# Cross attention by long convolution and a routed FFN on one core: count loads spread over the gathers, store ahead of the read-back, places behind a product

## What is computed

```python
x = x + long_convolution(layernorm(x), k, bias, ctx, ctx)      # stage 1
xt = layernorm(x).reshape(2048, 256)                           # stage 2: 16 experts, 4 a token
scores = softmax(xt @ Wg.T)
topi = 4 best experts within the 2 best groups of 4
h = silu(xt @ W1[e]) * (xt @ W3[e])                            # inner width 176
y = sum over the 4 chosen e of scores[e] * (h @ W2[e])
z = (silu(xt @ Ws1.T) * (xt @ Ws3.T)) @ Ws2.T                  # shared expert, width 352
x = x + y + z
```

## Time and profile before

| | us |
|---|---|
| median of 3 runs | 414.01 |
| lowest and highest of them | 413.64, 414.26 |
| the profiled execution's own time | 410.32 |
| its span, first to last instruction | 408.6 |

### The profile page before, as it was taken

How to read it: one execution, slowest core, us unless ns; L and a number is a source line. 1 busy time by engine, 2 the same in 40 slices (tenths; PEclk the granted TensorE clock), 3 DMA queues, 4 the chain that set the end, 5 groups by cost and what they waited for, 6 DMA issues and landing times.

```text
span 408.6 us, 9369 instructions
## 1 busy us (share of the span) xinstructions
PE 395.1 (97%) x2144; PEld 292.9 (72%) x2145; DVE 241.7 (59%) x663; ACT 168.0 (41%) x513; POOL 185.1 (45%) x231
## 2 busy tenths in 40 slices
PE   7999999999999999999999999999999999999994
PEld 6788788788888445555877777777676767677772
DVE  3576577898978447674344444464646464646464
ACT  5348557555653640111234334333343433333341
POOL 3253333338887644646463333333333333333344
PEclk9999999999999999999999999999999999999999
DMA  7964664468869996454443333646364645454662
GB/s 238 368 232 144 204 223 143 144 243 295 283 222 379 322 315 203 147 217 154 141 148 117 110 110 109 200 134 211 124 213 134 201 146 189 158 192 154 219 222 98
DMA packets 39421, 79.71 MB, mean 195 GB/s; under 512 B 5792, under 2 KB 26624, under 8 KB 37344
## 3 DMA queue, kind: packets, MB, share of 16 engines
q1 hardware_dynamic: 32528, 59.57, 44.5%
q0 software_dynamic: 6864, 19.80, 12.5%
HBM read 54.95 MB, written 24.40 MB: 194 GB/s over the span
## 4 chain that ended last, share of the span: by engine, by line
PE 69%; DVE 8%; DMA 7%; SPq 5%; issue 5%; POOL 3%; ACT 1%; DVEq 1%; POOLq 0%
PE heads L1189 17%; PE bank L1251 13%; PE heads L1097 9%; PE heads L1229 8%; PE bank L1241 5%; DMA toep<-rows_scratch 4%; PE heads L1099 4%; PE bank L1208 4%; DVE kv L636 3%; PE heads L1199 3%; PE bank L1111 3%; SPq L324 2%; DVE prod L665 2%; POOL rows_scratch L563 2%; DMA toep<-toep_in 2%
## 5 line engine op out<-in xcount | busy, mean ns | idle before, releaser
L617 POOL DMA_INDIRECT y_scratch<-toep,dest_i x79 | 76.6, 969 | 119.0 <-DVE dest_i L962 106.0
L1189 PE MATMUL heads<-w,toep 128*128 x316 | 106.6, 460 | 0.0
L1251 PE MATMUL bank<-w,toep 88*128 x316 | 82.0, 381 | 0.5 <-DVE toep L932 0.5
L563 POOL DMA_INDIRECT rows_scratch<-rows,slot_i x64 | 63.4, 991 | 38.9 <-issue 19.1
L1097 PE MATMUL heads<-toep,kv 128*128 128x256 f32 x256 | 77.8, 386 | 2.4 <-DVE kv L636 1.7
L1189 PEld LDWEIGHTS heads<-w,toep 128*128 128x128 f32 x316 | 53.8, 190 | 17.0
L458 ACT ACTIVATE toep<-heads 128x176 f32<-128x176 f32 x79 | 25.0, 317 | 82.9 <-PE heads L1189 82.9
L1251 PEld LDWEIGHTS bank<-w,toep 88*128 88x128 f32 x316 | 53.7, 190 | 6.1 <-issue 1.2
L932 DVE COPY toep<-heads 88x256 f32<-88x256 f32 x79 | 33.2, 421 | 37.9 <-PE heads L1199 37.8
L1099 PEld LDWEIGHTS heads<-toep,kv 128*128 128x128 f32 x256 | 48.6, 190 | 6.6
L665 DVE TENSOR_TENSOR prod<-heads,ctx_rep 128x1024 f32<-128x1024 f32 x32 | 39.0, 1219 | 22.2 <-PE bank L1111 19.8
(11 more groups left out here) (158 smaller groups left out, 439.8 us busy)
## 6 DMA issues: line engine op xcount, KB each, us to landing
ctx_rep<-ctxr_in SPq DMA_DIRECT2D x16, 1024.0 KB, 4.9
toep<-rows_scratch SPq DMA_DIRECT2D x79, 144.0 KB
prod<-y_scratch SPq DMA_DIRECT2D x7, 1024.0 KB, 5.2
w<-w_in SPq DMA_DIRECT2D x16, 352.0 KB
w<-w_in SPq DMA_DIRECT2D x16, 176.0 KB
rows_scratch<-pad_row SPq DMA_DIRECT2D x17, 144.0 KB
ctx_tr<-ctxt_in SPq DMA_DIRECT2D x16, 128.0 KB, 5.0
toep<-toep_in SPq DMA_DIRECT2D x4, 512.0 KB, 7.1
```

The costliest lines, as they stand in the source:

```text
L563: pool.indirect_dma_start(rows_d, bass.IndirectOffsetOnAxis(ap=slot_i[:, u, k:k + 1].bitcast(U32), axis=0), rows[:, u, :], None).then_inc( ...
L617: pool.indirect_dma_start(y_d, bass.IndirectOffsetOnAxis(ap=dest_i[b][:, 0:1].bitcast(U32), axis=0), y_sb[b], None).then_inc(y_sent[b], 16)
L1189: last = nc.tensor.matmul(up_ps[p], x_tr[p][:, blk, :], w13[:, bass.ds(e, 1), blk, :].rearrange("p a n -> p (a n)"), start=blk == 0, stop= ...
L1251: last = nc.tensor.matmul(dn_ps[p], hid_tr[p][:, c, :], w2[:, bass.ds(e, 1), c, :].rearrange("p a n -> p (a n)"), start=c == 0, stop=c == 1)
```

## The change

Two parts, independent of each other.

1. In SP's loop over m = 4 to 8, each of the gathers 8m to 8m + 3 is followed by the load of one of the four counts of sends. Behind them come the store and then the read-back, which finds its counts in registers and only waits and issues its DMA. Before, the store stood behind the gather 8m + 1, and the four loads and the read-back behind the gather 8m + 2. The other read-backs load their counts as before.
2. On DVE, `places(3)` stands behind `hidden_shared(5)` rather than ahead of it.

```diff
-            def read_back(i, u0, units, into, signal):
-
-                sends = [sp.value_load(tile_row[0:1, bass.ds(i * DEPTH + (TILES + b), 1)],
-                                       min_val=16, max_val=16 * (TILES // DEPTH)) for b in range(DEPTH)]
+            def sends_of(i, b):
+
+                return sp.value_load(tile_row[0:1, bass.ds(i * DEPTH + (TILES + b), 1)],
+                                     min_val=16, max_val=16 * (TILES // DEPTH))
+
+            def read_back(i, u0, units, into, signal, sends=None):
+
+                if sends is None:
+                    sends = [sends_of(i, b) for b in range(DEPTH)]
                 for b in range(DEPTH):
                     sp.wait_ge(y_sent[b], sends[b])
...
             with sp.Fori(4, 9) as m:
-                gathers(m, 0, 2)
+                sends = []
+                for b in range(DEPTH):
+                    gathers(m, b, b + 1)
+                    sends.append(sends_of(m - 3, b))
                 store(m - 4, m * 2 - 8, 2)
-                gathers(m, 2, 3)
-                read_back(m - 3, m * 2 - 6, 2, back, back_in)
-                gathers(m, 3, 8)
+                read_back(m - 3, m * 2 - 6, 2, back, back_in, sends)
+                gathers(m, 4, 8)
...
             marks(3)
+            hidden_shared(5)
             places(3)
-            hidden_shared(5)
             dve.wait_ge(counted, 1)
             slot_of_expert(3)
```

## The result

The changed kernel takes 417.98 us, the median of 5 runs (416.46 to 418.60), against 414.15 for the kernel before (5 runs, 413.64 to 415.31, the three of the table above among them). The ratio is 1.0083, with a 95% interval of 1.0056 to 1.0110: slower by 3.4 us (2.3 to 4.6), where the prediction had 0.9 and a range that ended at 416.7. The profiled execution spans 414.7 us, against 408.6.

The account below looks back on a forecast made before the run. The prediction took PE, busy for 97% of the span, to bound the kernel. Part 1's +0.25 us and part 2's 0.64 gave +0.9 on a median of 414.01, so 414.9 us, with a range of 412.5 to 416.7.

Parts of the forecast that it names:

- 3.5 us: Time PE loses over tiles 33 to 73, the five turns m = 4 to 8, 0.70 a turn.
- U: Start of the up product of tile 8m + 1; the turn's first add was forecast at U + 4.85.
- Restarting PE costs some 0.1 more: In each turn, PE's restart behind the late first add was put at 0.1 us beyond the lateness of 0.6.
- So 0.75 a turn: PE's loss in each turn under part 1, 0.70 to 0.80 us; 3.75 for five against 3.5 before.
- the first add must start by U + 4.23: Latest start of DVE's first add in a turn for copy_h to be ready for PE's down product.
- The 0.03 us of room: Before the change, DVE's first add in turn m = 4 starts at U + 4.20, against a limit of U + 4.23.
- up to 0.35: PE's restart behind the wait for the gather in turn m = 4, 1.01 lost less 0.66 us idle.
- PE loses another 0.64 us: Part 2: places(3) delays add_z(2), so PE waits 0.64 us longer ahead of the twelve down products.
- 0, if something on DVE gave way: Lower bound of part 2's cost ahead of the twelve down products; the upper was 0.75 us.
- The send is caught: Rival: POOL's send falls behind the read-back and place(33) waits for it; +2.65 us, 416.7, chance 0.17.
- The read-back fits: Rival: in the turns, DVE's late adds go unseen by PE or the read-back lands sooner; -1.9 us, 412.1, chance 0.20.
- Places hidden: Rival: PE's wait ahead of the twelve down products doesn't grow; +0.25 us, 414.3, chance 0.08.

Follow-up runs that it names:

- Experiment 3: Part 1 alone with DVE's four adds one step later: 0.9920 of the kernel before; the same adds on the kernel before: 1.0165.
- Experiment 5: PE loads the next tile's expert number earlier: on part 1 alone 0.9999 of the kernel before, on the kernel before 0.9964.
- part 1 alone: SP's loop as changed, places(3) at its old place, against the kernel before: 1.0059, 415.35 against 412.82 us.
- experiments 2 and 4: Part 1 alone, with store behind read-back: 1.0091 of the kernel before; loads paired behind two gathers: 0.9999; read-back ahead of gather 8m + 3: 0.9927.

## Why the prediction was wrong

*Right.* The bound was found: the 3.5 us lie in the turns, and behind PE's wait for the gather stands a second chain over DVE that ends at nearly the same time. Part 1 takes the first away and makes the second longer; PE's idle time moves from the turning (L1208) to the down product (then L1251, now L1258); the gather leaves 1.04 us behind `take`, where 1.1 was predicted; the first add starts at U + 4.92 on the mean, where U + 4.85 was. Experiment 3 confirms the chain: with the add off it, nothing is lost. That the add came within 0.07 us of its forecast is partly luck, see below.

*Wrong, and the step that failed: "Restarting PE costs some 0.1 more", "So 0.75 a turn".* The lateness of 0.6 was right (0.69 measured), the restart wasn't: 0.58 us beyond the lateness, 1.27 a turn. The price was taken from the twelve down products at 168.96, behind which no register is loaded. In a routed step PE's program loads an expert's number behind the stalled product. In the changed kernel that load and the step behind it cost 0.46 a turn (1.54 us from down product to up product rather than 1.18, and 0.10). Experiment 5 takes the load from behind the stall, and this cost is gone.

*A second error in the same step, "the first add must start by U + 4.23".* The due time left out the 0.24 us from the end of the copy to the loading of the weights. With it and the 1.92 in place of 2.05 it is U + 4.12, so the mean add was 0.80 late and not 0.69: 0.80 + 0.46 = 1.26 of the 1.27 that a turn loses. The 0.03 us of room was read from one turn as well. In the same trace the first adds of the other four turns start at U + 3.80, 4.06, 3.85 and 3.66.

*The nearer price.* The row that was nearest in kind was in sight: the stall for the gather cost "up to 0.35" beyond its idle time, and even that was set aside. In the five turns part 1 comes to +2.8 us on the two profiled executions, or +2.3 on the means of the profiles, in place of +0.25; part 1 alone measured +0.59% (0.32% to 0.86%), which is 1.3 to 3.6 us.

*Too small a sample: 3.5 us as what before loses.* A second profile loses 4.7. This goes the other way, and makes the surprise smaller, not larger.

*Part 2, "PE loses another 0.64 us".* In the first two profiles the wait grew by 0.89 (0.51 to 1.40), in all of them on the mean by 0.34 (1.06 to 1.40), and alone it measured 1.0004 (0.9988 to 1.0020), which holds both nothing and 0.64. The direction was right. The size was wrong because the execution that was read had the smallest wait of ten, with no gap on DVE at all; the bound "0, if something on DVE gave way" was the better half of the truth.

*A term that came out by two errors.* The read-back's issue was to start at U - 0.75 and, with the 0.38 us of the earlier trace rows, to end at U - 0.37. It ends within 0.03 us of U in all five turns, 0.35 to 0.4 later. (Its row starts at U - 0.53 and is 0.53 us long in one turn, and starts at U - 0.03 to U and is 0.02 long in the others; part 1 alone has both kinds with the same ends, so the end is the figure to go by.) SP's rows before it are in place: the store leaves 1.33 us behind the gather, where 0.65 + 0.35 + 0.34 had been put. In return the first add comes 4.65 to 4.87 us behind that end in four turns, rather than 5.6 - 0.38 = 5.2, and 5.48 behind it in turn m = 4. The read-back's packets take 3.5 to 3.7 us from first to last in these four turns, 3.4 to 3.8 in the kernel before, and 4.35 in turn m = 4: the overlap with the store, put at 0.3 a turn, shows in one turn alone. Why the issue ends later was not tried.

*The rivals.* "The send is caught" had the nearest size (416.7, inside the measured interval), but by luck, since its cause wasn't there: `place(33)` didn't wait. It did in experiments 2 and 4, where the read-back left before the send or within 0.1 us behind it. The prediction compared the ends of the two issues, where the starts of the packets decide: 1.54 us behind the send's row and 1.04 behind the read-back's. "The read-back fits" was wrong, as the add came 0.4 us or more behind even the U + 4.23. The 0.03 us of room that was named against it was the reading of one turn. "Places hidden" is what part 2 nearly does. The sum with the numbers measured since, +2.3 for part 1 and +0.34 for part 2, is +2.6, inside the measured interval of 2.3 to 4.6; the remaining 0.8 to its middle isn't accounted for.

## What to carry to other kernels

When two chains end within a few tenths of each other, relieving one gains nothing by itself: work out the due time of the other, with the time that the signal takes (0.24 us here) and from more than one turn, and move the work that has room (here DVE's adds by one step) together with the transfer. Price a stall by a stall at the same place of the same program, with all that the engine must do in order behind it, register loads among them, and hoist what doesn't depend on the wait. Before summing tenths of a microsecond from one profiled execution, read the same waits in a second one.

## What the runs showed that was not expected

- A stall of PE costs its lateness and no more where no register load stands behind it (0.91 us lost for 0.90 late). With the load in order it costs 0.34 to 0.66 us more (ten turns of two kernels), since the load begins 0.76 us behind the stalled product rather than beside it, and takes 0.3 us, in two turns of five 0.6.
- A 128 KB send in POOL's queue is held by the 1 MB read-back in SP's, even when its row starts 0.07 us ahead: its reader waited 1.78 us. Its first packet comes 1.54 us behind its row, the read-back's 1.04. With the read-back's issue ending 1.3 us behind the send's start, and a 256 KB store in front of it, the send was not waited for.
- DVE's idle time ahead of the same instruction in the same order of work was 0 to 1.13 us from one execution to another, and PE's wait behind it 0.51 to 1.70; with `places(3)` moved the two were 0.22 or 0.23 and 1.40 or 1.41 in all four profiles. The rows name different releasers for it (a product, "issue", "remote"); no run tells what it is.
- Moving DVE's adds one step later costs 1.65% in one order of SP's DMAs and gains 1.4% in the other.
